# A three-layer vision kernel: the attention stage's loop over images, with counts in registers, is written out with constants

## The chip, the cores and the metric

The kernel runs on one core of a Trainium2 chip. The metric is device time in microseconds, lower is better. The core has five engines that run their own instruction streams: TensorE (PE), VectorE (DVE), ScalarE (ACT), GpSimd (POOL) and SyncE (SP). They meet only at semaphores.

## The reference

The input x is (32, 64, 56, 56) in float32. Constants and helper functions are cut.

```python
x = x + conv3x3(group_norm(x), sign(weight))          # 64 channels, groups of 2
t = x as tokens                                       # (32, 3136, 64)
n = layer_norm(t)
Q, K, V = n @ W_q, n @ W_k, n @ W_v                   # 64 -> 32
w = softmax(Q @ K.T / sqrt(32))                       # 3136 x 3136 for each image
t = t + (w @ V) @ W_o + b_o + n
x2 = layer_norm(t)
gate = softmax(mean(x2, over images) @ Wr + br)       # 8 experts, one gate per token place
h = relu(bn(x2 @ W1 + b1)); h = relu(bn(h @ W2 + b2)) # for each expert
t = t + sum over experts of gate * (h @ Wo + bo)
```

## The kernel before

There are two stages in time. The attention stage takes every image through the convolution, both norms and the attention, keeps a running sum of the second norm's output, and stores t and x2 to HBM. The expert stage reads them back; the change doesn't touch it.

In the attention stage an image passes through four steps: normalize (statistics, padding), prepare (convolution, first norm, projections to Q and K, values), attend (scores, exponentials, sums, values, division) and norms (second norm). They are pipelined over images: one **slot** works at the same time on image i+3 in normalize, i+2 in prepare, i+1 in attend and i in norms. In attend there are 8 blocks of query columns (QC) times 25 blocks of 128 keys (KB). For each of the 200 pairs TensorE makes scores (L704), ACT takes the exponential (L650), and POOL adds three blocks of probabilities into one sum (L446, L449; L455 for the rest). TensorE multiplies the probabilities by the values (L713, L719) and the sums by ones (L715). Beforehand a maximum of each query row is needed: TensorE makes raw scores (L691), DVE reduces them (L504, L509, L514), and TensorE turns the negated maxima into a row (L697) that DVE copies next to Q (L520). L751 is the convolution, L783 the values' projection, L743 and DVE's L532 to L545 the group statistics.

The order in a slot is written by hand. `timeline` gives each piece of work a place between 0 and 200, and sorts them; `walk` goes through the sorted list on every engine, so each engine issues its share of the pieces in that order. `step` of each engine turns a piece into instructions and waits. Waits are on semaphores that are never reset: every wait names the total count that has to be reached, and the count depends on the image. `Image.count` makes it, and `Place` does so for the shared banks:

```python
def count(self, per, n):
    return self.c * per + n if self.t is None else self.t * (2 * per) + (self.c * per + n)
```

`t` is None in slots that are written out, and the count is then a constant. In the loop, t is the iteration's register, and the count is computed by the engine.

With 32 images there are three slots that fill the pipeline, then 28 slots in a loop of 14 iterations with two slots each (two, since buffers alternate with the image), and then a slot of all four steps with the last images, written out, and three that drain the pipeline. Each engine has this loop in its own program (L245); SP, which only stores and fetches, has its own (L399).

Of the kernel before, what the change touches and what calls it, by code (L numbers as in the profile page):

```python
# [150 lines left out]
def rows_needed(c):  # L151

    return -(-(c + 1) * 2 * QW // (P * MR))
# [59 lines left out]
def walk(engine, images, lag, step):  # L213

    order = timeline(lag)
    x_total = [0]

    def slot(normalize, prepare, attend, norms, t=None):
        stages = {"normalize": normalize, "prepare": prepare, "attend": attend, "norms": norms}
        uses, after, x_uses = {}, {}, {}  # L220
        for _, stage, kind, args in order:
            if stages[stage] is not None:
                if (stage, kind) in X_KINDS:
                    x_uses[stage, kind, args] = len(x_uses)
                if kind in ("proj", "max", "row"):
                    uses[kind, args] = len(uses)
                elif kind == "blockmax":
                    after[kind, args] = uses["max", (min(args[0] * MR + MR, KB) - 1, MC - 1)] + 1
                elif kind == "score" and args[1] == 0:
                    needed = rows_needed(args[0]) - 1  # L230
                    after[kind, args] = 0 if needed < AHEAD else uses["row", (needed,)] + 1
        at = attend if attend is not None else norms
        for _, stage, kind, args in order:
            if stages[stage] is not None:
                x_use = x_uses.get((stage, "project", args[:1]) if kind == "divide" else (stage, kind, args))
                place = Place(None if attend is None and norms is None else at, uses.get((kind, args)), after.get((kind, args)),
                              x_use, (t, x_total[0]))
                step(stage, kind, stages[stage], place, *args)
        x_total[0] += len(x_uses)

    slot(Image(0), None, None, None)
    slot(Image(1), Image(0), None, None)
    slot(Image(2), Image(1), Image(0), None)
    loops, x_first = (images - 4) // 2, x_total[0]
    with engine.Fori(0, loops) as t:  # L245
        x_total[0] = x_first
        for j in range(2):
            slot(Image(j + 3, t), Image(j + 2, t), Image(j + 1, t), Image(j, t), t)
    x_total[0] = x_first + 2 * N_X * loops
    slot(Image(images - 1), Image(images - 2), Image(images - 3), Image(images - 4))  # L250
    slot(None, Image(images - 1), Image(images - 2), Image(images - 3))
    slot(None, None, Image(images - 1), Image(images - 2))
    slot(None, None, None, Image(images - 1))


def attention_phase(nc, images, x, conv_w, w_q, w_k, w_v, w_o, b_o, ident_in, block_in, pair_in, t2_dram, x2_dram, ident, feat):
# [5 lines left out]
    with ctx:  # L262
# [87 lines left out]
        with nc.Block() as block1:  # L350
            @block1.sync
            def _(sp):
                def load(dst, src):
                    sp.dma_start(dst, src).then_inc(loaded_w, 16)
                sp.dma_start(conv_raw, conv_w.rearrange("o i a b -> o i (a b)")).then_inc(conv_loaded, 16)
                load(ident[:], ident_in)
                load(block[:], block_in)
                load(pair[:], pair_in)
                for h in range(2):
                    rows = slice(h * C, (h + 1) * C)  # L360
                    for r in range(4):
                        load(wq_st[rows, r, :], w_q)
                        load(wk_st[rows, r, :], w_k)
                    load(wv_st[rows, :], w_v)
                    load(bo_col[rows, :], b_o.rearrange("(c a) -> c a", a=1))
                sp.wait_ge(fills_done, 1)
                for j in range(GROUP):
                    load(wo_st[j * U:(j + 1) * U, :], w_o)

                def fetch(image):  # L370
                    n = image.number()
                    if image.c or image.t is not None:

                        sp.wait_ge(pad_hi, image.count(CH, 0))
                        sp.wait_ge(pad_lo, image.count(CH, 0))
                        sp.wait_ge(xn_ready, image.count(CH, 0))
                    src = x_flat[bass.ds(n, 1)].rearrange("i c n -> (i c) n")
                    for h in range(2):
                        sp.dma_start(xin[h * C:(h + 1) * C, :], src).then_inc(x_loaded, 16)
                    for h in range(2):  # L380
                        sp.dma_start(xpk[h * C:(h + 1) * C, :].rearrange("c (r w) -> c r w", w=HW),
                                     x_rows[bass.ds(n, 1), h].rearrange("i c r w -> (i c) r w")).then_inc(xpk_loaded, 16)

                def store(image):
                    n, par = image.number(), image.parity

                    def to(dram):
                        return dram[bass.ds(n, 1)].rearrange("i a c n -> (i a c) n")
                    sp.wait_ge(t2_ready, image.count(3 * QC, 3 * QC))
                    sp.dma_start(to(t2_dram), t2[:, par, :]).then_inc(t2_stored[par], 16)  # L390
                    sp.wait_ge(xn2_ready, image.count(CH, CH))
                    sp.dma_start(to(x2_dram), xn2[:]).then_inc(x2_stored, 16)

                fetch(Image(0))
                fetch(Image(1))
                fetch(Image(2))
                fetch(Image(3))
                loops = (images - 4) // 2
                with sp.Fori(0, loops) as t:  # L399
                    for j in range(2):  # L400
                        store(Image(j, t))
                        fetch(Image(4 + j, t))
                for n in range(images - 4, images):
                    store(Image(n))

                for j in range(2):
                    sp.wait_ge(t2_stored[j], 16 * images // 2)
                sp.wait_ge(x2_stored, 16 * images)

            @block1.gpsimd  # L410
            def _(gp):
# [16 lines left out]
                def step(stage, kind, im, place, *a):  # L428
# [34 lines left out]
                    elif (stage, kind) == ("norms", "apply"):  # L463
# [4 lines left out]
                        gp.tensor_tensor(piece(feat, q), piece(feat, q), piece(xn2, q), ALU.add).then_inc(feat_ready, 1)  # L468

                walk(gp, images, ACT_LAG, step)  # L470

            @block1.vector
            def _(dve):
# [25 lines left out]
                def step(stage, kind, im, place, *a):  # L499
# [92 lines left out]
                    elif stage == "norms" and kind == "mean":  # L592
# [5 lines left out]
                        v.tensor_tensor(piece(xn2, q), piece(t2[:, par, :], q), xb[:, 0:CW], ALU.subtract).then_inc(x_used, 1)  # L598

                walk(dve, images, DVE_LAG, step)  # L600

            @block1.scalar
            def _(act):
# [4 lines left out]
                def step(stage, kind, im, place, *a):  # L608
# [46 lines left out]
                    elif stage == "norms" and kind in ("mean", "var"):  # L655
# [4 lines left out]
                        elif kind == "var":  # L660
# [5 lines left out]
                            s.activation(rstd2[:, q % 2, :], rstd2[:, q % 2, :], ACT.Exp, scale=-0.5).then_inc(rstd2_ready, 1)  # L666

                walk(act, images, ACT_LAG, step)

            @block1.tensor  # L670
# [511 lines left out]
```

## Time and profile before

| | |
|---|---|
| time, median of 3 runs | 7569.28 us (7566.72 to 7577.81) |
| the profiled execution's own time | 7563.37 us |
| its span | 7561.7 us |
| PE busy | 7229.4 us, 96% |
| POOL busy | 5608.5 us, 74% |
| DVE busy | 5437.3 us, 72% |
| ACT busy | 4267.5 us, 56% |
| HBM traffic | 31 GB/s over the span |

All figures from the profile are of one execution. Busy time leaves out register, branch and semaphore instructions. "PEld" is the loading of weights, which overlaps the matmuls. The attention stage ends some 6250 us into the span, and the expert stage takes the rest.

### The profile page before, as it was taken

Reading aid. Unit: us, or ns where it says so; the run is one execution under the profiler, and the core shown is the slowest. Engines: PE = TensorE matmul, PEld = TensorE weight load, DVE = VectorE, ACT = ScalarE, POOL = GpSimd, SP = SyncE. Lnnn points to the kernel's source line nnn. Section 1 sums busy time; section 2 is a strip of 40 time slices with the busy share of each in tenths; the row PEclk is TensorE's granted clock in tenths of the full one; section 3 lists DMA queues with packets and bytes.
Section 4 is the critical chain, followed back from the end, with each engine's and each line's share of the span. In section 5 each row is a group of like instructions: output and inputs, shape, how many; then the busy total and the mean of one; then the engine's idle time right before and its main releaser. Section 6 shows DMA issues by size and latency. Waiting matters only on the chain. (4 is left out here: it accounts for less than half of the span.)

```text
span 7561.7 us, 162050 instructions
## 1 busy us (share of the span) xinstructions
PE 7229.4 (96%) x47378; PEld 3642.1 (48%) x47378; DVE 5437.3 (72%) x9566; ACT 4267.5 (56%) x9201; POOL 5608.5 (74%) x5524
## 2 busy tenths in 40 slices
PE   6999999999999999999999999999999987999999
PEld 4555555555555555555555555555555532333332
DVE  6787878787778787787877787878788723444444
ACT  1565656555555555555555555555556553555555
POOL 2888888888888888888888888888888881222222
PEclk7999999999999999999999999999999987999999
DMA  1011101011111111001011111101100002333333
GB/s 29 14 23 23 23 23 23 23 23 23 23 23 23 23 23 23 23 23 23 23 23 23 23 23 23 23 23 23 23 23 22 10 14 62 85 78 84 84 83 79
DMA packets 218262, 242.59 MB, mean 32 GB/s; under 512 B 147128, under 2 KB 200760, under 8 KB 213376
## 3 DMA queue, kind: packets, MB, share of 16 engines
q1 hardware_dynamic: 205184, 207.34, 11.5%
q0 software_dynamic: 12288, 25.71, 1.6%
q8 instruction: 375, 6.14, 0.3%
q14 instruction: 415, 3.40, 0.2%
HBM read 155.89 MB, written 77.07 MB: 31 GB/s over the span
## 5 line engine op out<-in xcount | busy, mean ns | idle before, releaser
L650 ACT ACTIVATE probs<-bank 128x392 f32<-128x392 f32 x6400 | 2809.1, 497 | 2022.2 <-PE bank L704 2001.0
L504 DVE TENSOR_REDUCE part_max<-bank 128x1 f32<-128x448 f32 x5600 | 3218.6, 612 | 629.8 <-PE bank L691 614.1
L446 POOL TENSOR_TENSOR psum<-probs 128x392 f32<-128x392 f32 x2048 | 2098.4, 1025 | 496.2 <-ACT probs L650 475.3
L691 PE MATMUL bank<-ks,qs 96*128 96x448 f32 x5600 | 2390.2, 431 | 78.2 <-DVE part_max L504 71.8
L449 POOL TENSOR_TENSOR psum<-psum,probs 128x392 f32<-128x392 f32 x2048 | 2099.9, 1025 | 267.8 <-ACT probs L650 101.6
L704 PE MATMUL bank<-qs,ks 97*128 97x392 f32 x6400 | 2040.5, 369 | 69.1 <-issue 47.1
L713 PE MATMUL bank<-probs,vs 128*32 128x392 f32 x12288 | 1775.8, 509 | 21.9 <-POOL psum L449 12.4
L715 PE MATMUL bank<-psum,ones 128*32 128x392 f32 x4096 | 1748.3, 509 | 0.0
L691 PEld LDWEIGHTS bank<-ks,qs 96*128 96x128 f32 x5600 | 1065.8, 190 | 1380.0 <-DVE part_max L504 819.6
L704 PEld LDWEIGHTS bank<-qs,ks 97*128 97x128 f32 x6400 | 1188.7, 190 | 468.9 <-ACT probs L650 249.7
L1055 DVE SCALAR_TENSOR_TENSOR h<-ebank,tmp_n,gate_w 128x784 f32<-128x784 f32 x512 | 529.3, 1034 | 645.6 <-PE ebank L1108 645.6
L1041 ACT ACTIVATE h<-ebank,tmp_c,tmp_s 128x392 f32<-128x392 f32 x1024 | 637.5, 673 | 535.0 <-PE ebank L1094 534.4
L1018 POOL DMA_DIRECT2D out_dram<-fin x256 | 181.5, 712 | 880.8 <-DVE fin L1068 874.8
L713 PEld LDWEIGHTS bank<-probs,vs 128*32 128x32 f32 x12288 | 309.9, 108 | 573.4 <-issue 492.9
L584 DVE RECIPROCAL rden<-bank 128x98 f32<-128x98 f32 x512 | 384.7, 757 | 218.0 <-PE bank L727 218.0
L1094 PE MATMUL ebank<-xs,w1f 64*64 64x392 f32 x4096 | 464.5, 526 | 0.0
L1119 PE MATMUL ebank<-h,w3f 128*64 128x392 f32 x2048 | 450.0, 518 | 2.8 <-DVE h L1055 2.8
L1108 PE MATMUL ebank<-h,w2f 64*64 64x392 f32 x4096 | 436.5, 495 | 9.6 <-DVE h L1055 8.4
L751 PE MATMUL bank<-pad,conv_st 128*128 128x392 f32 x1536 | 329.0, 366 | 10.3 <-POOL pad L438 8.8
L751 PEld LDWEIGHTS bank<-pad,conv_st 128*128 128x128 f32 x1536 | 306.7, 202 | 16.7 <-POOL pad L438 10.3
L715 PEld LDWEIGHTS bank<-psum,ones 128*32 128x32 f32 x4096 | 282.4, 108 | 0.0
L455 POOL TENSOR_TENSOR psum<-psum,probs 64x392 f32<-64x392 f32 x256 | 260.4, 1017 | 22.2
(133 smaller groups left out, 5787.3 us busy)
## 6 DMA issues: line engine op xcount, KB each, us to landing
xin<-in_x_dram SPq DMA_DIRECT2D x64, 784.0 KB, 8.5
xs<-x_dram SPq DMA_DIRECT2D x512, 98.0 KB, 2.4
xpk<-in_x_dram SPq DMA_DIRECT2D x64, 392.0 KB, 11.9
t_dram<-t SPq DMA_DIRECT2D x32, 784.0 KB, 11.7
x_dram<-xn SPq DMA_DIRECT2D x32, 784.0 KB, 3.6
res<-t_dram SPq DMA_DIRECT2D x256, 98.0 KB, 2.5
out_dram<-fin POOLq DMA_DIRECT2D x256, 98.0 KB, 2.5
w1f<-in_L_ffn_W_dram SPq DMA_DIRECT2D x2, 128.0 KB
```

Of the source, the lines that this page charges most:

```text
L446: gp.tensor_tensor(into, one, two, ALU.add).then_inc(sum_part, 1)
L449: add = gp.tensor_tensor(into, into, three, ALU.add)
L504: v.tensor_reduce(part_max[:, b, m:m + 1], m_bank[place.bank()][:, 0:MW], AX.X, ALU.max).then_inc(m_used, 1)
L650: s.activation(probs[:, held(c, k), :], s_bank[n % 3][:, 0:2 * QW], ACT.Exp, scale=SCALE).then_inc(p_ready, 1)
L691: mm(m_bank[place.bank()][:, 0:MW], qs[par][0:KS, b * P:(b + 1) * P], ks[par][0:KS, m * MW:(m + 1) * MW], start=True, stop=True).then_inc( ...
L704: mm(s_bank[(c * KB + k) % 3][:, 0:2 * QW], ks[par][0:KS + 1, k * P:(k + 1) * P], qs[par][0:KS + 1, c * 2 * QW:(c + 1) * 2 * QW], start=Tr ...
L713: mm(o_bank[n * U:(n + 1) * U, 0:2 * QW], vs[par][:, GROUP * r + n, :], probs[:, held(c, GROUP * r + n), :], start=r == 0, stop=False)
L715: mm(o_bank[GROUP * U:P, 0:2 * QW], ones[:], psum[:, (c * ROUNDS + r) % SUMS, :], start=r == 0, stop=r + 1 == ROUNDS)
L751: last = mm(xb[:, 0:CW].rearrange("p (r w) -> p r w", w=HW), conv_st[:, r, dx, :], pad[:, top:top + 2 * CP - 1:2, dx:dx + HW], start=r + d ...
L1041: last = s.activation(h1[:, n % 2, j, :], a_bank[n % 2][:, j, 0:CW], ACT.Relu, bias=tmp["c1"][:, at:at + 1], scale=tmp["s1"][:, at:at + 1])
L1055: v.scalar_tensor_tensor(h2[:, n % 2, :, :], bank2[:, :, 0:CW], tmp["n2"][:, e:e + 1], gate_w[:, e:e + 1, :].broadcast_to([P, 2, CW]), ALU ...
L1094: last = mm(bank[out, half, 0:CW], w1f[rows, of, :], xs[rows, 2 * p + side, :], start=True, stop=True)
```

## The change

Both loops, the one in `walk` and SP's, become loops of the program that writes the kernel, so that their 14 iterations are written out one behind another. `t` is then a plain number in each, and so is every count.

```diff
@@ walk @@
     loops, x_first = (images - 4) // 2, x_total[0]
-    with engine.Fori(0, loops) as t:
+    for t in range(0, loops):
         x_total[0] = x_first
         for j in range(2):
             slot(Image(j + 3, t), Image(j + 2, t), Image(j + 1, t), Image(j, t), t)
@@ attention_phase, sync @@
                 loops = (images - 4) // 2
-                with sp.Fori(0, loops) as t:
+                for t in range(0, loops):
                     for j in range(2):
                         store(Image(j, t))
                         fetch(Image(4 + j, t))
```

No operation on data and no transfer is added, removed or put in another order. What goes are the branches, and the register instructions (REGISTER_ALU) of the loop's body, which each iteration ran: in the program's text 1051 become 25 on TensorE, 504 become 20 on DVE, 514 become 21 on ACT, 437 become 3 on POOL and 8 become 3 on SP. The matmuls in TensorE's text go from 4122 to 21438.

The instructions of TensorE where an iteration ends, before the change. `ident_r,neg_max` is the row of maxima, `qs,ks` the scores; the names in brackets are the semaphores that a row waits for.

```order
L694 REGISTER_ALU
L202 REGISTER_ALU [waits negmax_ready]
L697 MATMUL bank<-ident_r,neg_max 97x128 [waits m_used]
L697 MATMUL bank<-ident_r,neg_max 97x128 x3
L245 REGISTER_ALU
L245 COMPARE_AND_BRANCH
L704 MATMUL bank<-qs,ks 128x392 [waits p_ready,m_used]
L713 MATMUL bank<-probs,vs 32x392 [waits sum_ready]
```

Behind the branch stands the slot that follows the loop. When the branch is taken, TensorE goes on here instead, at the top of the body:

```order
L245 ISA
L202 ISA [waits m_used]
L704 MATMUL bank<-qs,ks 128x392 [waits p_ready]
L710 ISA
L713 MATMUL bank<-probs,vs 32x392 [waits sum_ready]
L713 MATMUL bank<-probs,vs 32x392 x2
L715 MATMUL bank<-psum,ones 32x392
L202 REGISTER_ALU
```

After the change TensorE has this at each of these places:

```order
L704 MATMUL bank<-qs,ks 128x392 [waits p_ready] x3
L697 MATMUL bank<-ident_r,neg_max 97x128 [waits m_used,negmax_ready]
L697 MATMUL bank<-ident_r,neg_max 97x128 x3
L704 MATMUL bank<-qs,ks 128x392 [waits p_ready,m_used]
L713 MATMUL bank<-probs,vs 32x392 [waits sum_ready]
L713 MATMUL bank<-probs,vs 32x392 x2
L715 MATMUL bank<-psum,ones 32x392
L691 MATMUL bank<-ks,qs 128x448 [waits m_used]
```

The matmuls are the same in number and order; branch and register rows between them are gone, as they are already behind the loop's exit.

POOL at the sums of one column block, inside the loop before the change (`psum` is the sum, `probs` the probabilities):

```order
L445 REGISTER_ALU
L446 TENSOR_TENSOR psum<-probs 128x392 [waits p_ready]
L447 REGISTER_ALU
L448 REGISTER_ALU [waits p_ready]
L449 TENSOR_TENSOR psum<-psum,probs 128x392 [waits sum_part]
L452 REGISTER_ALU
L453 REGISTER_ALU [waits p_ready]
L455 TENSOR_TENSOR psum<-psum,probs 64x392 [waits sum_part]
```

And after it:

```order
L435 TENSOR_SCALAR xin<-xin,gs,gb 128x784 [waits pad_hi]
L438 TENSOR_TENSOR pad<-xin,pad 64x14x56 [waits pool_chain]
L446 TENSOR_TENSOR psum<-probs 128x392 [waits p_ready,pad_lo]
L449 TENSOR_TENSOR psum<-psum,probs 128x392 [waits sum_part,p_ready]
L455 TENSOR_TENSOR psum<-psum,probs 64x392 [waits sum_part,p_ready]
```

The register rows are gone, and the wait for `p_ready`, which the second of them carried, has moved into the add itself, beside that for `sum_part`.

## Rows read from the trace of the kernel before

**Rows 1.** The page: busy time, and TensorE's granted clock in 40 slices.

```profile
PE 7229.4 (96%) x47378; PEld 3642.1 (48%) x47378; DVE 5437.3 (72%) x9566; ACT 4267.5 (56%) x9201; POOL 5608.5 (74%) x5524
PEclk7999999999999999999999999999999987999999
```

**Rows 2.** Timeline of PE at slot ends: start, duration in us, instructions, idle time before.

```profile
356.89 0.48 PE L697 MATMUL bank<-ident_r,neg_max 128*97 128x128 f32 x4
...
733.00 0.55 PE L697 MATMUL bank<-ident_r,neg_max 128*97 128x128 f32 x4 [0.23 <-DVE neg_max L514]
...
926.29 0.55 PE L697 MATMUL bank<-ident_r,neg_max 128*97 128x128 f32 x4 [0.25 <-DVE neg_max L514]
...
1114.40 0.47 PE L697 MATMUL bank<-ident_r,neg_max 128*97 128x128 f32 x3 [0.22 <-DVE neg_max L514]
...
5499.91 0.55 PE L697 MATMUL bank<-ident_r,neg_max 128*97 128x128 f32 x4 [0.22 <-DVE neg_max L514]
...
5688.06 0.55 PE L697 MATMUL bank<-ident_r,neg_max 128*97 128x128 f32 x4 [0.25 <-DVE neg_max L514]
...
5875.72 0.48 PE L697 MATMUL bank<-ident_r,neg_max 128*97 128x128 f32 x4
```

**Rows 3.** Waits of PE in the loop (357 to 5689): us in total, times, longest.

```profile
PE bank L704 <- issue: 47.1, 13, 3.9
```

**Rows 4.** Timeline of PE, first L704 behind a branch back and behind the exit.

```profile
737.46 0.69 PE L704 MATMUL bank<-qs,ks 97*128 97x392 f32 x1 [3.91 <-issue]
...
5689.40 0.44 PE L704 MATMUL bank<-qs,ks 97*128 97x392 f32 x1 [0.79 <-DVE qs L520]
```

**Rows 5.** Windows: us, busy of PE, PEld, DVE, ACT, POOL; PE clock, DMA, GB/s.

```profile
735.70:742.50 6.80, 5.04 (x18) 3.40 (x19) 0.62 (x1) 0.50 (x1) 5.26 (x6) 0.50 0.02 6
...
193.00:733.00 540.00, 526.29 (x3333) 285.01 (x3326) 438.68 (x809) 322.69 (x730) 471.54 (x458) 1.00 0.10 21
...
3975.00:3980.00 5.00, 3.92 (x21) 2.79 (x21) 1.56 (x3) 1.61 (x4) 4.76 (x6) 0.84 0.00 0
```

**Rows 6.** Windows of a slot in the loop and of the slot behind it.

```profile
545.00:733.00 188.00, 183.57 (x1154) 99.82 (x1155) 151.17 (x277) 112.50 (x255) 164.87 (x161) 1.00 0.10 23
...
5688.00:5876.00 188.00, 182.97 (x1158) 100.41 (x1158) 149.21 (x277) 112.47 (x255) 163.09 (x159) 1.00 0.10 22
```

**Rows 7.** L783 on PE in three slots: duration ns min/median/max, first and last start.

```profile
L783 PE MATMUL bank<-xn,wv_st x16: 480/507/533, 5565.1 to 5567.3; 64*32 64x384 f32 x12, 64*32 64x416 f32 x4
...
L783 PE MATMUL bank<-xn,wv_st x16: 479/507/533, 5753.2 to 5755.4; 64*32 64x384 f32 x12, 64*32 64x416 f32 x4
...
L783 PE MATMUL bank<-xn,wv_st x16: 479/507/533, 5940.8 to 5943.0; 64*32 64x384 f32 x12, 64*32 64x416 f32 x4
```

**Rows 8.** DVE groups by form, 357:5688, then 5688:5876: busy us, mean ns.

```profile
L540 DVE TENSOR_TENSOR gvar<-gm,gsq 128x1 f32<-128x1 f32 x28 | 26.2, 936 | 1.0
...
L540 DVE TENSOR_TENSOR gvar<-gm,gsq 128x1 f32<-128x1 f32 x1 | 0.2, 159 | 0.0
```

**Rows 9.** Waits of PE and of POOL from 5688 to 5876.

```profile
PE bank L713 <- POOL psum L455: 0.8, 1, 0.8
...
POOL psum L446 <- ACT probs L650: 11.0, 14, 1.7
```

**Rows 10.** Timeline of POOL, one pair of adds in either form.

```profile
5614.41 1.01 POOL L446 TENSOR_TENSOR psum<-probs 128x392 f32<-128x392 f32 x1
5615.50 1.03 POOL L449 TENSOR_TENSOR psum<-psum,probs 128x392 f32<-128x392 f32 x1
...
5802.81 1.02 POOL L446 TENSOR_TENSOR psum<-probs 128x392 f32<-128x392 f32 x1
5803.97 1.04 POOL L449 TENSOR_TENSOR psum<-psum,probs 128x392 f32<-128x392 f32 x1
```

**Rows 11.** DMA queues, 357:733, then 5688:6100: packets, MB, share of 16 engines.

```profile
q8 instruction: 22, 0.36, 0.4%
...
q8 instruction: 21, 0.34, 0.4%
```

## The prediction, made before the changed kernel ran

> **What bounds the kernel now.** I began with the page. TensorE is busy for 96% of the span and its granted clock is at the upper level nearly throughout [rows 1]. Next I wanted the length of one slot. In the middle of the attention stage a slot is one image at each of four stages, 1154 matmuls [rows 6]. The last matmuls of a slot are four of L697, so the timeline of TensorE at the slot ends gives the lengths [rows 2]. The loop begins at 356.89 and ends at 5688.06: 28 slots in 5331.2 us. They come in two kinds. The slot in the middle of an iteration takes 188.1 us (926.29 to 1114.40). One that begins an iteration takes 193.3 us (733.00 to 926.29), with the same work. Yet the loop's very first iteration, which is entered and not branched back to, takes 376.1 us for its two slots (356.89 to 733.00), 188.05 each. So the extra 5.2 us belong to the branch back.
>
> What they are is seen in the waits of TensorE over the loop: "issue", thirteen times, 47.1 us in all and 3.9 at most, always ahead of L704 [rows 3]. Fourteen iterations have thirteen branches back. The timeline at one of them has L704 begin at 737.46 after 3.91 us of such idle time. At the loop's exit, where the branch is not taken, the same matmul waits 0.79 us, and for DVE's row copy [rows 4]. So a branch costs TensorE 3.9 less 0.8, some 3.1 us, of bare waiting. The rest is the clock: the windows show 0.50 granted, the 1.2 GHz level, from 735.7 to 742.5, and 5.04 of these 6.80 us are matmuls [rows 5]. At half the speed they did in 5.0 us what takes about 2.5 at the upper level, which is more than the 2.1 us that are left to explain. From 193 to 733, straight-line code and the first iteration, the clock was 1.00 throughout.
>
> **What the change takes away.** (1) The thirteen stalls, with their slow clock. Nothing takes their place: the slots without a branch have the same data waits and none of this. By the whole loop it is 5331.2 - 28 x 188.05 = 65.8 us; thirteen times 5.2 is 67.6. Some slow clock may come back. A slot that no branch preceded had it once, 0.84 granted in 3975 to 3980 [rows 5]; I leave 1 us for more of these.
>
> (2) The register instructions. For each wait on a count that depends on the iteration an engine first computes the count. What they cost I take from a slot that exists in both forms. The slot after the loop, 5688.06 to 5875.72, is written out already, has all four stages, the same matmuls in the same order, and constants. It took 187.66 us [rows 2], 0.39 less than 188.05. Its TensorE is busy 182.97 us against 183.57, its DVE 149.21 against 151.17 [rows 6]. The gain isn't spread: up to the values' matmuls (L783) the two forms need 65.1 and 65.2 us (5565.1 less 5499.91; 5753.2 less 5688.06) [rows 7]. So register work as such is hidden, by engines that run ahead of their waits. The difference comes later, where DVE takes tiny operations between its maxima: L540 on 128x1 took 936 ns in the loop, in the mean of 28, and 159 ns in the slot written out [rows 8]. The 0.8 us between are most of a POOL operation, whose length is 1.02 [rows 10]: with waits computed in another way, POOL and DVE meet at another moment. The Trainium skill, page Advanced Engine Details and Errata, section GPSIMD Details, says that the Pool engine shares a read and a write interface with DVE and conflicts with DVE instructions that have two SBUF inputs; L540 is one, and the row agrees.
>
> Is that to be counted 28 times? The meeting depends on a phase of some tenths of a us. But slots repeat with great regularity, and all 28 in the loop had the long form, as their mean shows. Bounds: 0 (the luck of one slot) and 28 x 0.39 = 10.9 us. I take the upper one, since the code and its surroundings are the same as they will be in the other slots.
>
> (3) POOL pays. In its sums the second add now waits in itself for the probabilities, and the wait on the first add becomes a separate one. Starts of L446 and L449 lie 1.09 us apart in the loop (5614.41, 5615.50) and 1.16 in the slot written out (5802.81, 5803.97) [rows 10]. With 8 x 8 such pairs per slot that is 0.07 x 64 = 4.5 us more on POOL, and there TensorE does wait for it, 0.8 us at L713 [rows 9]. This is in the 187.66 already. What is not in it is a lag carried into the next slot. But POOL's idle time ahead of L446 in the written-out slot is still 11.0 us [rows 9], and the slot behind it reaches L783 at 5940.8, 65.1 us after 5875.72 [rows 7], as any other. The lag is gone by then, so I add nothing.
>
> (4) Instruction fetch. The program of TensorE grows fourfold. But the loop fetches as it is: the main instruction queue moved 0.36 MB in the 376 us of the first iteration, and 0.34 MB in 412 us of the straight-line code behind the loop [rows 11]. A body that stayed on the core would move none. So the written-out program fetches about as much per slot as now. I price it at 0, hidden beside the matmuls as it is there; without that cover a stop would cost what a branch does, 3.1 us and up.
>
> The Trainium skill, page Runtime: NRT & Kernel Launch, section Instruction fetch mechanics, says that a taken branch whose target is outside the current window forces a fetch before execution goes on, while straight-line code streams by itself. The stall at the taken branch and its absence at the exit [rows 4] agree with it.
>
> (5) SP's loop: its waits and transfers keep their order, and it touches the same data at the same points; the slots as they are wait for none of it. 0.
>
> Sum: 65.8 + 10.9 - 1 = 75.7 us. Against the profiled execution, 7563.4 (span 7561.7 and 1.7 around it), that is 7487.7. The three runs lie at 7566.7 to 7577.8, median 7569.3, 5.9 us above the profiled one; from them it would be 7493.6. Part of their scatter is probably that of the stalls, so I forecast between the two, **7490 us**, 1.0% below before.
>
> **The rivals.** A, as summed, 7487 to 7494: 0.57.
>
> B, only the stalls go, and slots keep 188.05: 7563.4 - 64.8 = 7498.6, or 7504.5 from the median. For it: the gain of the written-out slot stands on one specimen, and behind that image no more inputs are fetched. Against: the 0.39 us came from DVE and POOL, not from a transfer. 0.25.
>
> C, more than the sum: phases fall better than in the specimen. DVE's busy time fell by 2.0 us there and TensorE's slot by only 0.4; another 0.5 a slot would be 14 us more, 7474. 0.10.
>
> D, the stalls aren't the branch's: something stops TensorE every so many instructions, and does so without the loop as well. Then 10.9 us or nothing is gained: 7552 to 7563. Against it are the count, 13 and none elsewhere [rows 3], and the exit without a stall [rows 4]. 0.05.
>
> The Trainium skill, page Advanced Engine Details and Errata, section Control Flow Timing, has a compare-and-branch at about 108 ns. By that alone the thirteen would be worth 1.4 us and the time 7562, within D; the row with 3.91 us speaks against it.
>
> E, slower: POOL becomes what ends last, in the second half of a slot, where it has norms, sums and padding. If the 4.5 us of (3) reached TensorE in every slot, 28 x 4.5 = 126 against 75.7 gained: 7614. It decides once POOL's idle time ahead of L446, 11.0 us a slot, is used up, and outweighs the gain from 2.7 us a slot on; now 0.8 is seen. 0.03.
>
> **The numbers.** The range runs from between C and A to beyond the dearer end of B, 7480 to 7507. It holds A, B and a fifth of C, some 0.84; the rest of C, D and E are left out. A measurement of this kernel can tell 0.2%, 15 us, from no change. Faster: A, B, C and a little of E: 0.93. Within 0.2%: D, less a bit, 0.04. Slower: 0.03.
>
> **What would show it.** In the profile after: no "issue" wait at L704 in the attention stage; slot ends (L697) 187.7 us apart all along, and no pair of 188 and 193; the granted clock at 1.00 in windows like 735 to 743; L540 near 160 ns in all slots, L449 1.16 us behind L446, POOL's idle time at L446 at some 11 us a slot. Slots of 188.05 with L540 at 936 ns would be B. "Issue" stalls at other places would be D. A wait of L713 for POOL that grows beyond 0.8 us a slot would be E. What lies behind the last loop slot, 7561.7 - 5688.1 = 1873.6 us, should stay; if it moves, the sum lacks a part. The likeliest way to be wrong is that slots of the written-out program depend on their history in a way that one specimen doesn't tell.

## The result, and the profile after

The changed kernel takes 7484.98 us in the median of four runs (7483.23 to 7491.41), against 7573.55 us before in four (7566.72 to 7578.8). The ratio is 0.9885, with a 95% interval of 0.9868 to 0.9902. The forecast was 7490 us, range 7480 to 7507. The profiled execution took 7484.78 us, with a span of 7482.9: 78.8 us less span than before.

The page, busy time and TensorE's granted clock in 40 slices, beside [rows 1]:

```profile
PE 7175.7 (96%) x47378; PEld 3627.8 (48%) x47378; DVE 5378.6 (72%) x9566; ACT 4265.1 (57%) x9201; POOL 5602.3 (75%) x5524
PEclk7999999999999999999999999999999988999999
```

The timeline of PE at slot ends, to be held against [rows 2]:

```profile
356.77 0.48 PE L697 MATMUL bank<-ident_r,neg_max 128*97 128x128 f32 x4
...
544.28 0.48 PE L697 MATMUL bank<-ident_r,neg_max 128*97 128x128 f32 x4
...
731.78 0.48 PE L697 MATMUL bank<-ident_r,neg_max 128*97 128x128 f32 x4
...
919.54 0.48 PE L697 MATMUL bank<-ident_r,neg_max 128*97 128x128 f32 x4
920.81 0.45 PE L704 MATMUL bank<-qs,ks 97*128 97x392 f32 x1 [0.79 <-DVE qs L520]
...
5609.35 0.48 PE L697 MATMUL bank<-ident_r,neg_max 128*97 128x128 f32 x4
```

The 28 slots take 5609.35 - 356.77 = 5252.6 us instead of 5331.2, 187.59 each. There are no longer two kinds: 187.51, 187.50 and 187.76 us lie between the first four rows. L704 behind a slot end now waits 0.79 us for DVE's row copy everywhere, as it did at the loop's exit [rows 4]. 187.59 is the mean. It is to be held against 188.11, the mean of the 14 slots of the kernel before that no branch back preceded and in which the clock stayed up; the first two, by which the prediction went, take 188.05. The thirteen slots behind a branch back take 192.05 to 193.69 us there, 192.94 in the mean. All of the gain is here: behind 5609.35 there are 1873.6 us, as before.

The waits of PE in these slots (us in total, times, longest), where [rows 3] had 47.1 us of issue:

```profile
PE bank L691 <- DVE part_max L504: 42.0, 119, 0.8
PE bank L713 <- POOL psum L455: 23.1, 27, 1.1
PE bank L704 <- DVE qs L520: 22.1, 28, 0.8
PE bank L713 <- POOL psum L449: 13.5, 53, 0.3
```

There is no issue wait among them, and there is a new one: 36.6 us in which L713 waits for POOL. The instruction queue moved 4.23 MB in these slots, where it moved 5.47 MB before. The windows of one slot and of the whole stretch show the clock:

```profile
732.00:920.00 188.00, 182.89 (x1158) 100.20 (x1156) 149.32 (x277) 112.80 (x256) 164.98 (x161) 1.00 0.10 22
...
1984.00:1989.00 5.00, 4.78 (x22) 2.46 (x22) 3.75 (x8) 1.88 (x4) 4.70 (x5) 0.66 0.00 0
357.00:5608.00 5251.00, 5114.23 (x32304) 2801.84 (x32307) 4173.46 (x7756) 3150.52 (x7111) 4611.35 (x4480) 1.00 0.10 22
```

The granted clock is 1.00 over the 5251 us. It still fell once in a while by itself, as in 1984 to 1989 (0.66).

DVE's small operations over the 28 slots (busy us, mean ns), beside [rows 8]:

```profile
L538 DVE TENSOR_TENSOR gsq<-gm 128x1 f32<-128x1 f32 x28 | 19.4, 691 | 1.0
L545 DVE TENSOR_TENSOR gb<-gsq,gs 128x1 f32<-128x1 f32 x28 | 16.5, 588 | 1.0
L532 DVE SCALAR_TENSOR_TENSOR mv<-mv 128x1 f32<-128x1 f32 x28 | 6.5, 233 | 0.0
L540 DVE TENSOR_TENSOR gvar<-gm,gsq 128x1 f32<-128x1 f32 x28 | 4.5, 159 | 1.0
```

L540 is at 159 ns in all 28, and L532, which took 855 ns in the mean before the change, at 233. L538 stays long (724 before), and L545, which took 159 ns before, now takes 588. So the four together went from 2.67 to 1.67 us a slot: only part of the long forms is gone. The timeline of POOL has a pair of adds 1.17 us apart, beside [rows 10]. That is also the median of all 1792 pairs in the slots; before the change it is 1.10:

```profile
5526.58 1.03 POOL L446 TENSOR_TENSOR psum<-probs 128x392 f32<-128x392 f32 x1
5527.75 1.02 POOL L449 TENSOR_TENSOR psum<-psum,probs 128x392 f32<-128x392 f32 x1
```

### The profile page after: what moved, and what is told of

Same layout as the page of the kernel before. It is cut to its first block and busy times, and to the rows that moved or that the text cites. A ratio compares the mean times of both kernels' runs of the same rounds, so it can differ in the third digit from the quotient of the medians.

```text
span 7482.9 us, 130695 instructions
## 1 busy us (share of the span) xinstructions
PE 7175.7 (96%) x47378; PEld 3627.8 (48%) x47378; DVE 5378.6 (72%) x9566; ACT 4265.1 (57%) x9201; POOL 5602.3 (75%) x5524
## 5 line engine op out<-in xcount | busy, mean ns | idle before, releaser
L446 POOL TENSOR_TENSOR psum<-probs 128x392 f32<-128x392 f32 x2048 | 2104.0, 1027 | 340.4 <-ACT probs L650 325.2
L704 PE MATMUL bank<-qs,ks 97*128 97x392 f32 x6400 | 2036.9, 368 | 32.1 <-DVE qs L520 25.3
L713 PE MATMUL bank<-probs,vs 128*32 128x392 f32 x12288 | 1768.6, 507 | 59.0 <-POOL psum L455 32.5
L704 PEld LDWEIGHTS bank<-qs,ks 97*128 97x128 f32 x6400 | 1188.2, 190 | 428.9 <-ACT probs L650 206.0
L713 PEld LDWEIGHTS bank<-probs,vs 128*32 128x32 f32 x12288 | 310.3, 108 | 621.7 <-issue 466.2
L751 PEld LDWEIGHTS bank<-pad,conv_st 128*128 128x128 f32 x1536 | 290.2, 191 | 16.7 <-POOL pad L438 10.3
L455 POOL TENSOR_TENSOR psum<-psum,probs 64x392 f32<-64x392 f32 x256 | 260.1, 1016 | 36.7
```

The source lines that it names most:

```text
L446: gp.tensor_tensor(into, one, two, ALU.add).then_inc(sum_part, 1)
L704: mm(s_bank[(c * KB + k) % 3][:, 0:2 * QW], ks[par][0:KS + 1, k * P:(k + 1) * P], qs[par][0:KS + 1, c * 2 * QW:(c + 1) * 2 * QW], start=Tr ...
L713: mm(o_bank[n * U:(n + 1) * U, 0:2 * QW], vs[par][:, GROUP * r + n, :], probs[:, held(c, GROUP * r + n), :], start=r == 0, stop=False)
```

## The experiments

Each kernel differs from the one before the change or from the changed one by the edit shown, and was timed in rounds with the kernel before, whose median lay between 7568 and 7569.5 us in all of them. "Short slot" is a slot behind no branch back, and "collision" is short for a DVE operation that takes long while POOL is adding. A profile is of one execution, so slot lengths come from one execution each; where a mean over short slots is given, single slots with a spell of slow clock are left out. In kernels whose text got eight lines longer, L705 is what L697 was, L712 was L704 and L721 was L713.

**1. TensorE alone is written out.**

```diff
+def iterations(engine, loops, written):
+    if written:
+        yield from range(loops)
+    else:
+        with engine.Fori(0, loops) as t:
+            yield t
...
-    with engine.Fori(0, loops) as t:
+    for t in iterations(engine, loops, written):   # written: True on TensorE only
```

> Only TensorE's loop is written out; DVE, ACT, POOL and SP keep theirs, with registers and branches. Theory (the long slots are TensorE's own stall at its branch, with the slow clock behind it; registers are hidden; the short collisions of DVE with POOL hang on DVE's and POOL's code): the 5.2 us at 13 places go, up to 0.8 us at each may come back because another engine is late after its own branch, L540 stays at 936 ns and slots stay at 188.05 to 188.1. Span 7561.7 - 65.8 = 7496, up to 7507. Rival (every engine's branch costs that engine about as long as TensorE's, and they only lie side by side now): the other engines' stalls show up in TensorE's waits, 2 to 3 us at each of 13 places, span 7520 to 7535.

Measured: 7497.16 us, ratio 0.9909 (0.9892 to 0.9925). PE's timeline at slot ends, and its waits:

```profile
355.89 0.48 PE L705 MATMUL bank<-ident_r,neg_max 128*97 128x128 f32 x4
...
919.80 0.56 PE L705 MATMUL bank<-ident_r,neg_max 128*97 128x128 f32 x4
1107.83 0.56 PE L705 MATMUL bank<-ident_r,neg_max 128*97 128x128 f32 x4
...
5620.16 0.56 PE L705 MATMUL bank<-ident_r,neg_max 128*97 128x128 f32 x4
```

28 slots in 5264.3 us, 188.0 each, and no issue wait of PE. So 66.9 of the 78.6 us come from TensorE's own program. A short slot is 188.01 us in the mean, 0.1 less than before, so TensorE's register instructions make up to 2.7 of the 66.9, and the stalls with their clock some 64.

The other engines still branch back here, and the trace shows that they do stop. From the branch to the next instruction of the loop pass 2.8 to 3.1 us on DVE, 2.4 to 2.7 on ACT and 2.5 to 2.8 on POOL, against 3.6 to 4.1 on TensorE in the kernel before. At the first branch back POOL's timeline goes on with the first of these rows, and DVE's with the second:

```profile
742.02 1.02 POOL L454 TENSOR_TENSOR psum<-probs 128x392 f32<-128x392 f32 x1 [1.84 <-issue]
```

```profile
735.66 0.62 DVE L512 TENSOR_REDUCE part_max<-bank 128x1 f32<-128x448 f32 x1 [2.53 <-PE bank L699]
```

So the rival was right that every engine has its stall, and wrong that TensorE would have to wait for them: none shows in its waits or in the slots' length.

**2. All but TensorE are written out** (the same edit, the other way round).

> The counterpart: DVE, ACT, POOL and SP written out, TensorE keeps loop, registers and branches. Theory: 13 issue waits of 3.5 to 3.9 us and slots of 193 us stay; L540 falls to some 160 ns, and slots without a branch take 187.5 to 187.7 instead of 188.1. 28 x 0.45 = 12.6 us gained, span 7549. Rival (TensorE's own register instructions cost it the 0.45 us a slot): slots stay at 188.1 and the span at 7562.

Measured: 7542.65 us, ratio 0.9966 (0.9953 to 0.9978). Waits of PE, then its slot ends:

```profile
PE bank L712 <- issue: 43.5, 13, 3.7
```

```profile
357.55 0.48 PE L705 MATMUL bank<-ident_r,neg_max 128*97 128x128 f32 x4
...
545.16 0.48 PE L705 MATMUL bank<-ident_r,neg_max 128*97 128x128 f32 x4
...
5671.06 0.48 PE L705 MATMUL bank<-ident_r,neg_max 128*97 128x128 f32 x4
```

The first short slot is 187.61 us, the mean of them 187.66, 0.07 more than in the changed kernel, and L540's counterpart is at 160 ns. The thirteen stalls stay. 28 slots take 5313.5 us, 17.7 less than before where 12.6 was expected: the slots with a stall also got shorter, by 0.8 us in the mean.

**3. Loops kept, with four slots in a body** (in the counts 2 becomes 4, and seven iterations).

```diff
-    loops, x_first = (images - 4) // 2, x_total[0]
+    loops, x_first = (images - 4) // 4, x_total[0]
...
-        for j in range(2):
+        for j in range(4):
```

> The loops stay on all engines, but a body has four slots and there are seven iterations: six branches back instead of thirteen, and as many register instructions executed as before. Theory: 7 x 5.2 = 36 us gained, span 7525; six issue waits at L704, slots without a branch at 188.1, L540 at 936 ns. Rival (the time goes with the number of register instructions): nothing gained, 7562.

Measured: 7537.68 us, ratio 0.9961 (0.9947 to 0.9975). A wait of PE:

```profile
PE bank L704 <- issue: 21.9, 6, 3.9
```

Six stalls instead of thirteen, each as long as before (3.65 us in the mean against 3.62) although the body is twice as long. The time goes with the number of branches back. The rival, that it goes with the number of register instructions, is out. The gain fell short: 28 slots take 5299.0 us, 32.2 less than before where 36 was expected. The 5.2 us of the expectation were above the mean of before, 4.8 (192.94 less 188.11), and the six long slots take 193.5.

**4. The changed kernel, POOL's waits exchanged** (likewise at L455).

```diff
-                        gp.wait_ge(p_ready, im.count(QC * KB, first + 3))
                         gp.wait_ge(sum_part, im.count(QC * (ROUNDS + 1), rounds + c + 1))
+                        gp.wait_ge(p_ready, im.count(QC * KB, first + 3))
                         add = gp.tensor_tensor(into, into, three, ALU.add)
```

> The changed kernel, with the two waits ahead of POOL's second and third add exchanged in the code, so that the wait for the first add stands inside the instruction again and that for the probabilities ahead of it. Theory: L449 begins 1.09 us after L446 again instead of 1.16, POOL falls less behind, and TensorE's waits at L713 for POOL (36.6 us in 28 slots) shrink below 10. If nothing else changes that is up to 27 us, span 7456. But the moments at which DVE meets POOL move too: if L540 and L532 are caught again (936 and 855 ns), slots go back to 188.05 and the span to 7495. I expect the second, 0.6 to 0.4. Rival (the POOL lag is no cause of the waits at L713): they stay at 36 us whatever the order.

Measured: 7487.02 us, ratio 0.9898 (0.9881 to 0.9914). POOL's timeline, then DVE's groups:

```profile
3008.36 1.01 POOL L446 TENSOR_TENSOR psum<-probs 128x392 f32<-128x392 f32 x1
3009.45 1.02 POOL L449 TENSOR_TENSOR psum<-psum,probs 128x392 f32<-128x392 f32 x1
```

```profile
L540 DVE TENSOR_TENSOR gvar<-gm,gsq 128x1 f32<-128x1 f32 x28 | 26.2, 937 | 1.0
L532 DVE SCALAR_TENSOR_TENSOR mv<-mv 128x1 f32<-128x1 f32 x28 | 25.3, 903 | 0.0
```

The pair is back at 1.09 us, no wait of L713 for POOL is left in PE's list, and the collisions are back. The slot is 187.76 us. One cost took the place of the other, as expected; only its size was not: not 188.05, but 0.3 less.

The starts of the 200 L704 of a slot, read from the traces and averaged over the slots, show where the two costs lie. At 116 us into a slot, ahead of DVE's small operations, the changed kernel and this one are within 0.03 us of each other. At 165 us the changed kernel is 1.3 us ahead, by its shorter DVE operations. At 187 us the two are level again, and what lies between is the stretch in which L713 of the changed kernel waits for POOL. So in the change itself fewer collisions gave 1.3 us a slot, and the longer pair of adds took them back.

**5. The kernel before, the same two waits exchanged.**

> The kernel before, loop and registers kept, with the two waits ahead of POOL's second and third add exchanged: the wait for the first add goes ahead of the instruction, that for the probabilities stands inside it. Theory (the 0.4 us a slot come from the moment at which POOL and DVE meet, set by the form of POOL's waits, not from the registers' absence): L449 begins some 1.16 us after L446, L540 falls to 160 ns, TensorE waits for POOL at L713 for over 1 us a slot, slots without a branch take 187.5 to 187.7; thirteen issue waits stay; span 7549. Rival (the registers cost it): slots stay at 188.1, span 7562.

Measured: 7559.41 us, ratio 0.9986 (0.9977 to 0.9996). In the loop the exchange works the other way, since the first wait is a register instruction's. PE's waits, POOL's timeline, DVE's group:

```profile
PE bank L713 <- POOL psum L455: 20.7, 27, 0.9
PE bank L713 <- POOL psum L449: 18.8, 48, 0.4
```

```profile
3007.30 1.03 POOL L446 TENSOR_TENSOR psum<-probs 128x392 f32<-128x392 f32 x1
3008.48 1.02 POOL L449 TENSOR_TENSOR psum<-psum,probs 128x392 f32<-128x392 f32 x1 [0.16 <-POOL psum L446]
```

```profile
L540 DVE TENSOR_TENSOR gvar<-gm,gsq 128x1 f32<-128x1 f32 x27 | 4.3, 159 | 0.9
```

Signs right, sum wrong: the collision goes and POOL's lag comes, but short slots stay near 188.1 (925.53 to 1113.70 is 188.17, the mean 188.14). So neither the theory (187.6) nor the rival (collisions as before) was right, and the 0.4 us of the changed kernel were not the collision's net. The median of the runs is 9.6 us less, which the slots don't explain. Some 3 us of it lie behind them: the written-out slots there got the quicker pair by the exchange, and from the last slot of the loop to the end it is 1870.6 us against 1873.6. In all fourteen traces that stretch takes 1867 to 1871 us where the waits are exchanged and 1873 to 1877 where they aren't. The rest stays open.

**6. The kernel before, three DVE instructions with one tensor input.**

```diff
-v.scalar_tensor_tensor(mv2[:, 1:2], mv[:, 0:1], mv[:, 0:1], mv[:, 1:2], ALU.mult, ALU.add)
+v.tensor_scalar(mv2[:, 1:2], mv[:, 0:1], mv[:, 0:1], mv[:, 1:2], ALU.mult, ALU.add)
-v.tensor_tensor(gsq[:, 0:1], gm[:, 0:1], gm[:, 0:1], ALU.mult)
+v.tensor_scalar(gsq[:, 0:1], gm[:, 0:1], gm[:, 0:1], None, ALU.mult)
-v.tensor_tensor(gvar[:, 0:1], gm[:, 1:2], gsq[:, 0:1], ALU.subtract)
+v.tensor_scalar(gvar[:, 0:1], gm[:, 1:2], gsq[:, 0:1], None, ALU.subtract)
```

> The kernel before with L532, L538 and L540 as tensor_scalar with one tensor input and the other operands as per-partition scalars; same results. Theory (DVE instructions with two tensor inputs in SBUF wait for a POOL instruction under way, others don't): the three take 150 to 250 ns instead of 855, 724 and 936 though POOL keeps its moments, and L449 stays 1.09 us behind L446. DVE is late for TensorE in just that stretch, so a slot gets 1.0 to 1.8 us shorter; 28 x 1.4 = 39 us, span 7523. Rival (it is the moment alone, any DVE instruction is held there): durations and slots unchanged, span 7562.

Measured: 7489.07 us, ratio 0.9895 (0.9879 to 0.9912), twice the expected gain, with loops, branches and registers all in place. DVE's groups, then PE's slot ends:

```profile
L532 DVE TENSOR_SCALAR mv<-mv 128x1 f32<-128x1 f32 x28 | 7.4, 266 | 0.0
L540 DVE TENSOR_SCALAR gvar<-gm,gsq 128x1 f32<-128x1 f32 x28 | 6.0, 215 | 1.0
L538 DVE TENSOR_SCALAR gsq<-gm 128x1 f32<-128x1 f32 x28 | 6.0, 214 | 1.0
```

```profile
545.46 0.48 PE L697 MATMUL bank<-ident_r,neg_max 128*97 128x128 f32 x4
731.02 0.48 PE L697 MATMUL bank<-ident_r,neg_max 128*97 128x128 f32 x4
921.78 0.48 PE L697 MATMUL bank<-ident_r,neg_max 128*97 128x128 f32 x4
```

A short slot takes 185.56 us instead of 188.1: the collisions cost 2.5 us a slot, a third more than the 1.8 by which the three instructions got shorter. (The slot behind a branch takes 190.76.) By the starts of L704, 1.6 of the 2.5 us are gained while DVE does these operations and 0.9 behind 165 us into the slot; what makes the second part isn't shown.

**7. The changed kernel with the same one-input forms.**

> The changed kernel with the same three instructions in one-input form. Only L538 was still long there (691 ns). Theory: it falls to about 150 ns; the slot is by now paced by POOL's lag in its second half (36.6 us of waits at L713), so little comes out: 187.59 falls by 0 to 0.4, span 7472 to 7483. Rival (DVE is still what TensorE waits for): 0.5 us a slot, 7469 or less.

Measured: 7485.94 us, ratio 0.9891 (0.9875 to 0.9908), and the 28 slots take 5254.5 us. L538 fell to 214 ns and nothing came of it, as the theory had it at its lower end. But it was not the only long one: L545, still with two inputs, went from 588 to 851 ns, so the four operations together got only 0.13 us shorter.

```profile
L545 DVE TENSOR_TENSOR gb<-gsq,gs 128x1 f32<-128x1 f32 x27 | 23.0, 851 | 0.9
```

**8. Both: waits exchanged and one-input forms, on the changed kernel.**

> Both edits on the changed kernel: waits exchanged and one-input forms. Theory: POOL's lag is gone as in the run with waits exchanged, and so are the collisions, so both of the costs that until now took each other's place are away: slots of 186.0 to 186.8 us against 187.59 and 187.76, span 7440 to 7462. Rival (the two don't add, something else ends last): 187.4, span 7478.

Measured: 7418.05 us, ratio 0.9800 (0.9784 to 0.9817). PE's slot ends:

```profile
359.96 0.56 PE L697 MATMUL bank<-ident_r,neg_max 128*97 128x128 f32 x4
...
545.45 0.48 PE L697 MATMUL bank<-ident_r,neg_max 128*97 128x128 f32 x4
...
5549.78 0.48 PE L697 MATMUL bank<-ident_r,neg_max 128*97 128x128 f32 x4
```

185.35 us a slot, 2.2 less than the changed kernel. The expectation had the sign and half the size.

L545 takes 412 ns here, so against number 7 two things changed, POOL's pace and L545. The starts of L704 tell them apart: number 7 is 0.6 us behind this one at 130 us into a slot, where L545 is, but only 0.2 at 165, and 2.2 at the end. So 2.0 of the 2.2 us arise in the last 20 us of the slot, where L713 waits for POOL in number 7 and not here.

**9 and 10. One engine written out alone:** POOL, with its waits exchanged so that the pair keeps 1.09 us, and DVE.

> The kernel before with POOL's loop alone written out, and POOL's waits exchanged so that the pair of adds keeps its 1.09 us. So POOL loses its register instructions and nothing else of the order of waits changes. In four runs so far with collisions and POOL's pace equal, the fully written-out form is 0.25 to 0.3 us a slot shorter, and TensorE's own part of that was 0.03. Theory: POOL, the engine with the least slack, is where the rest comes from; slots without a branch take 187.75 to 187.85, 13 issue waits stay, L540 stays at 936 ns; span 7554. Rival (it is DVE's register instructions): 188.05 to 188.1, span 7562.

> The kernel before with DVE's loop alone written out. Theory (POOL's register instructions cost the 0.3 us): slots without a branch stay at 188.05 to 188.1; L449 stays 1.09 us behind L446; span 7561. Rival (DVE's do): 187.75 to 187.85, span 7554.

Measured: POOL 7552.41 us, ratio 0.9980 (0.9970 to 0.9989); DVE 7570.08 us, ratio 1.0005 (0.9995 to 1.0014). A short slot of the first is 187.86 us (924.01 to 1111.87; the mean is 187.88), of the second 188.1 to 188.2, but for one of 189.6. So POOL's loop written out gives 0.23 us a slot, and DVE's gives nothing. (Of the 16 us by which POOL's runs are shorter, some 5 lie behind the slots, as in number 5.) Writing out POOL's loop takes away its register instructions and also puts its waits into other instructions; which of the two gives the 0.23 us isn't shown. ACT was not written out alone.

**11. Number 8 with L545 in one-input form too.**

> The kernel with waits exchanged and one-input forms, and L545 in one-input form as well; it took 412 ns in the mean there. Theory: it falls to some 214 ns, 0.2 us less of DVE in a stretch where TensorE still waits for DVE 29 us in 28 slots: 0 to 0.2 us a slot, span 7414 to 7420. Rival (this stretch no longer ends last): no change.

Measured: 7415.51 us, ratio 0.9799 (0.9783 to 0.9815). L545 fell from 412 to 214 ns, and the slots take 185.4 us as they did. The difference to number 8 is within the spread of the runs; L545 does not set a slot's length here.

**12. The kernel before with both edits of numbers 5 and 6.**

> The kernel before with both edits of its own: POOL's waits exchanged, which is the slower form in the loop (L449 1.18 us behind L446), and the one-input forms. It is the last of the combinations. Theory (a slot is paced by POOL where its pairs take 1.16 us or more, and by DVE's collisions where they take 1.09; the two don't add): slots without a branch take 187.9 to 188.2 in spite of the one-input forms, TensorE waits for POOL at L713 some 40 us in 28 slots, span 7556 to 7563. Rival (the collisions cost 2.4 us a slot by themselves, whatever POOL does): 185.7, span 7491.

Measured: 7557.42 us, ratio 0.9984 (0.9974 to 0.9993). Waits of PE:

```profile
PE bank L713 <- POOL psum L455: 21.0, 27, 0.9
PE bank L713 <- POOL psum L449: 19.5, 48, 1.3
```

The same one-input forms that gave 80 us in number 6 give nothing where POOL's pair takes 1.18 us. (L545 takes 904 ns here, as in number 7.) The slot behind the loop, written out, has the exchange's other form, and shows the same within one trace: it takes 185.38 us here, with a pair of 1.10 us, and 187.71 in number 6, with 1.17. The short slots of the eight combinations in one place:

| | pair of adds 1.09 us | pair 1.16 us or more |
|---|---|---|
| loop, two-input forms | 188.1 (before) | 188.1 (number 5) |
| loop, one-input forms | 185.6 (6) | 188.1 (12) |
| written out, two-input forms | 187.76 (4) | 187.59 (changed kernel) |
| written out, one-input forms | 185.35 (8) | 187.66 (7) |

The last is 5254.5 us over 28; without one slot of 190.62 with slow clock it is 187.55. A slot is short only where POOL's pair is quick and DVE isn't held; either alone costs nearly all of the 2.2 to 2.5 us.

## Why the prediction was right, and where it wasn't

The likeliest case, A, came nearest: the 7484.98 us lie 2 us below its bounds of 7487 to 7494, and 75.7 us were summed where 78.8 came off the span. Part of the agreement is luck, since two costs that the sum didn't name cancelled each other.

**The stalls, 65.8 us.** They measure some 64: thirteen times 4.8 us, and 1.4 for the slot of 189.5 with slow clock that the 65.8 also held. Number 1, where TensorE alone is written out, gains 66.9, TensorE's registers included. It shows that the other engines' stalls, which exist, cost nothing. Number 3 shows that each belongs to a branch back. Rival D, that something stops TensorE every so many instructions, is out by both.

**Registers and phase, 10.9 us.** They measure some 14: 28 times the 0.52 us between 188.11 and 187.59. It was read from a slot that already had the new form, and its 187.66 us became 187.59 in 28; the short slots of before were taken at 188.05 instead of 188.11. (Its own rows had a little of it: up to L783 the slot in the loop takes 5565.1 - 5499.91 = 65.2 us and the written-out one 65.1; the text has the two the other way round.) So the net was right to 4 us. The working behind it was not. The step that failed is "register work as such is hidden": it is on DVE (number 10), but writing out TensorE's loop gives 0.1 us a slot (number 1) and POOL's 0.23 (number 9). With pace and forms equal, the written-out kernel is 0.35 us shorter with two inputs (188.11 to 187.76) and 0.24 with one (185.59 to 185.35). And the attribution of the gain to L540 named one half of an exchange: fewer collisions gave 1.3 us a slot, and the longer pair of adds cost as much (number 4). Only 0.2 us of the 0.52 are left to it.

**"POOL pays", 0.8 us in a slot.** Mis-sized. The waits of L713 are 1.3 us a slot, and without them and the collisions a slot is 2.2 us shorter (number 8). The slot written out in the kernel before already had the 1.3, as there is a second row beside that of [rows 9]:

```profile
PE bank L713 <- POOL psum L449: 0.5, 2, 0.3
```

So the text had E announced by waits beyond 0.8, and they were beyond without E coming true: the slot's own 187.66 us had them in. POOL's idle time ahead of L446 is 9.0 us a slot (252.2 in 28), not 11. That no lag is carried into the next slot held: all 28 are alike.

**Fetch, 0.** Held: there is no issue wait of TensorE in the 28 slots. **Slow clock, 1 us.** About right: it came back for moments like that at 1984, and one slot takes 188.33 us.

**The forecast's time.** The median of before was put 5.9 us above the profiled execution, and half of that was taken off. The changed kernel's runs lie within 0.2 us of its profiled one in the median. So of the 5.0 us by which the forecast is high, 2.3 are that half, and 2.9 are the gain that the sum lacked. The runs of before spread over 12 us, those of the changed kernel over 8. That the stalls make the larger part of the spread was assumed and isn't shown: numbers 2 and 3, with stalls, spread over 10 us, and number 7, without, over 10 as well.

## What to carry over

When part of a loop exists in both forms in the same trace, measure the two and take the difference; it gives the net even where the account of its parts is wrong. But a net near zero can be two costs that hide each other: on this kernel both had to go at once, and the pair of edits was worth 67 us more, most of what the whole change gave. So look at what becomes late when a wait is folded into an instruction, before counting the removed instructions.

The fastest version found is the changed kernel with POOL's two waits exchanged and one-input forms for DVE's small operations: 7415.51 to 7418.05 us, 2.0% below before.

## What the runs showed of the hardware

- A branch back costs TensorE 3.0 to 4.1 us of issue wait where the trace has 2308 or 4616 matmul rows in the body. DVE, ACT and POOL stop for 2.4 to 3.2 us at theirs; on this kernel that stays hidden behind their slack (number 1). In the expert stage, whose innermost loop has a body of 160 matmul rows, the kernel before has 0.6 us of issue waits of PE in 1231 us, and from a branch back to the next instruction pass at most 0.3 us on any engine. The Trainium skill, page Runtime: NRT & Kernel Launch, section Instruction fetch mechanics, has the stall for targets outside the current window; both halves agree, though a body between these sizes wasn't tried.
- Two waits ahead of a POOL instruction are not alike. With the wait for the preceding POOL instruction inside it the next starts 1.10 us after the start of the last, and with it outside 1.17 (constants) to 1.18 (registers), in the median of some 1790 pairs each, for operations of 1.02 us. Which wait gets inside depends on the order in the code and on whether counts are constants.
- A DVE operation on 128x1 with two tensor inputs takes 159 ns, and up to 941 when POOL is at work. Every long one of L532, L538, L540 and L545 ends 11 to 26 ns after a POOL instruction does, in all 28 slots of the kernel before and of the changed one. As one tensor input with per-partition scalars it takes 214 ns and isn't held: L538 of number 7 ends 0.4 us before the POOL instruction beside it does. This agrees with what page Advanced Engine Details and Errata of the Trainium skill, section GPSIMD Details, states of two SBUF inputs. So semaphores are not the only place where engines meet, as the description of the core has it: DVE and POOL also meet here.
